# A two-block transformer on one core: the last attention group takes the middle token tiles of all heads first, and their feed-forward is queued between the outer tiles' attention

## The chip, the core and the metric

The kernel runs on one core of a Trainium2 chip. Its time is the device time of one execution in microseconds; the median of three runs is 643.6 (642.69 to 645.32). Times inside the kernel come from one profiled execution of it and are counted from the start of its span.

## The reference

x is 1024 tokens by 256 values. Four layers follow one another, each `x = x + f(layernorm(x))`: an attention over channels, a gated feed-forward with silu, a causal attention with 32 query heads of 64 and 8 key/value heads (rotary positions), and a feed-forward with quantised values and weights of -1, 0 and 1. The last two matter here:

```python
scores = jnp.where(causal, einsum('bhqd,bkhd->bhqk', xq, xk) * scale, -inf)
out = einsum('bhqk,bkhd->bqhd', softmax(scores), xv) @ wo           # the third layer
h = gelu(bitlinear(x, w_fc))                                        # the fourth layer, 256 -> 1024
x = x + bitlinear(h, w_proj)                                        # 1024 -> 256
def bitlinear(x, w):   # layer norm, quantised by the row's largest value, times ternary weights
    xn = layer_norm(x)
    return einsum('bsd,od->bso', absmax_quant(xn), ternarize_weights(w))
```

Both quantisations and both layer norms work on one token's row, so a token tile can go through the feed-forward as soon as its own x is complete, that is, when the output projections of all 32 heads have been added to it.

## The kernel before, in words

Tokens lie in eight tiles of 128. Every engine has its program written out in order (a `@block` per engine); semaphores are all that joins them, and each engine takes its own instructions strictly as written. The places where the order is set are the loops over `G` and the straight lists behind them.

The causal attention has 64 steps `G`, eight per key/value group `g`. A step takes two heads (pair `p` of the group) and two query tiles: part 0 is tile 4+r with 5+r key blocks, part 1 is tile 3-r with 4-r key blocks, nine blocks in all for each head, whatever r is (`of_step`, `blocks`). In a group, steps 0 to 3 take pair 0 with r = 0 to 3 and steps 4 to 7 take pair 1 in the same order. So a tile's heads are complete only in the second half of a group: the middle tiles (2 to 5, from r = 0 and 1) with step 5.

In a step PE computes the scores (`scores`, L1404), DVE the row maxima (L1005), ACT the exponentials (`exp_unit`, L661) and their rounding to fp16 (`p_high`, L670), POOL the rest (`p_low`, L497), SP issues two transposing DMAs (`pT_hi` at L376, `pT_lo` at L380, 18 blocks each), and three steps later PE multiplies with the values (`pv`, L1421 and L1425, 54 products), and DVE divides by the row sums (`normalise_o`, L1012, L1014). The table `JOBS` puts side work between the parts of a step: `q1t`, `kt`, `q0t` and `r` prepare the next group, `ot0` to `ot3` transpose the normalised outputs (PE L1436, ACT `oT_high` L642, DVE `oT_low` L1020; one `ot` covers two steps), `wo0` to `wo3` are the output projections (`out_project`, 12 products per tile pair j, all by the helper `product`, L1151) of the group before, added to x by DVE (`add_out`, L1026). `RING` assigns them two PSUM banks, 6 and 7, by turns; a job waits until the one two places ahead of it has been read (`emptied`). The weights of the projection are split in `wo_hi` (ACT L624) and `wo_lo` (POOL L476, between the halves of the last step's `p_low`).

Behind the loop PE has: pV of step 61, pV of 62, `ot2`, the projections j = 1 and 2 (tiles 2 to 5), pV of 63, `ot3`, the projections j = 0 and 3, then for the feed-forward four transposed y tiles (`x_transposes(3, ...)`, L1167), and a pipeline over tiles t: `fc(t)` is 8 products of 512 columns (L1151), 256 to 1024 values; ACT `gelu_of(t)` (L717), `centre(t)` (L725), `squares(t)` (L732); DVE quantises z (`tensor_reduce` L1131, then L1133 to L1135); PE `z_transposes(t)` (L1523); ACT `z_high` (L710) and DVE `z_low` (L1116) split the transposed z, and `pj(t)` is 16 products of 256 columns (L1151), whose result DVE adds to x (`result`, L1123, L1126). Buffers of gelu, z and zT are double, the one of the z transposes (banks 4 and 5) is single: `z_transposes(t)` waits for `z_low(t-1)`. POOL computes the means and inverse deviations (L455, L457, L529 to L537). PE's order there, with `fc` two tiles ahead of the transposes:

```python
            for t in range(NT):
                if t + 2 < NT:
                    fc(t + 2)
                z_transposes(t)
                if t >= 1:
                    pj(t - 1)
```

Before it DVE does the moments and the quantisation of y in halves of four tiles (`quantise`, L1077 to L1090), ACT `x_high` (L552) and DVE `y_low` (L1097) split the transposed y.

Of the kernel before, what the change touches and what calls it, by code (L numbers as in the profile page):

```python
# [31 lines left out]
def transformer_program(nc, x_in, wq_a, wk_a, wv_a, wo_a, w_gate_up, w_down,  # L32
# [97 lines left out]
    y = sb("y", 26, [NT, C], F32)  # L130
    yT_hi = sb("yT_hi", 34, [KC, T], F16)
# [33 lines left out]
    with ExitStack() as ctx:  # L165
# [117 lines left out]

        def owner(G, name):

            g = G // 8
            if name[:2] == "wo" or name in ("ot2", "ot3"):
                return g - 1
            return g if name[:2] in ("ot", "q1") else g + 1

        def job(G, slot):
# [3 lines left out]
            name = JOBS[G % 8][slot]  # L295
# [107 lines left out]
        def _(pool):  # L403
# [142 lines left out]
        @block.scalar
        def _(act):
# [1033 lines left out]
```

## Time and profile before

| | us |
|---|---|
| median of three runs | 643.6 |
| the profiled execution | 642.03 |
| its span | 640.2 |
| mean granted clock of TensorE, of full speed | 0.976 |
| PE busy | 573.9 |
| DVE / ACT / POOL busy | 462.9 / 436.1 / 453.3 |

The profiled execution's own time is its span and 1.8 us around it. "Releaser" in a row is what ended the idle time before an instruction. A chain of waits is read backwards from the last instruction: each piece is work that, had it been shorter, would have let the next begin earlier. PE's matmuls overlap, so a group of n of them starts its followers n times their spacing later, and a single one's mean is longer than that spacing.

### The profile page before, as it was taken

What the parts mean: (1) busy time and instruction counts of PE and PEld (TensorE: products, weight loads), DVE (VectorE), ACT (ScalarE), POOL (GpSimd) and SP (SyncE); (2) the same over time, 40 slices, a digit from 0 to 9 for tenths busy, and PEclk for the clock granted to TensorE, in tenths of its full rate; (3) what the DMA queues carried; (4) which work ended last, traced back from release to release, by engine and by line L of the source; (5) the groups of instructions that cost most, each with busy time, mean ns of one, the idle gap of its engine ahead of it and who ended that gap; (6) DMA issues with size and microseconds to landing.
All of it is one profiled execution on the core that took longest, in us unless ns stands there. A gap on an engine that the chain in (4) does not pass through costs nothing.

```text
span 640.2 us, 16852 instructions
## 1 busy us (share of the span) xinstructions
PE 573.9 (90%) x7136; PEld 485.6 (76%) x7136; DVE 462.9 (72%) x764; ACT 436.1 (68%) x600; POOL 453.3 (71%) x387
## 2 busy tenths in 40 slices
PE   6999999978889999999999999999999978674896
PEld 5878889857668888888787888888888767673475
DVE  4785766867668778777787877877787756518696
ACT  1624311368788797898888879779888878701794
POOL 5044435529999999998997998899799778533121
PEclk9999999999999999999999999999999989957899
DMA  8150004008999999999999999999999999960001
GB/s 286 57 184 0 2 22 87 1 22 148 174 187 209 186 200 191 185 186 196 197 191 186 189 180 202 194 188 193 186 188 171 184 193 186 184 132 1 1 25 42
DMA packets 317195, 91.79 MB, mean 143 GB/s; under 512 B 305984, under 2 KB 316224, under 8 KB 317120
## 3 DMA queue, kind: packets, MB, share of 16 engines
q1 hardware_dynamic: 317120, 90.72, 80.0%
q8 instruction: 56, 0.92, 0.5%
q14 instruction: 19, 0.16, 0.1%
HBM read 13.11 MB, written 1.05 MB: 22 GB/s over the span
## 4 chain that ended last, share of the span: by engine, by line
PE 34%; POOL 26%; DMA 16%; DVE 9%; SPq 6%; ACT 6%; issue 4%; POOLq 0%; ACTq 0%; DVEq 0%
POOL p_lo L497 19%; DMA pT_lo<-p_lo 15%; PE PS L1151 12%; SPq L376 4%; PE PS L1404 4%; PE PS L1284 3%; POOL roped L486 3%; PE PS L1421 3%; SPq L380 2%; POOL roped L483 2%; PE PS L1261 2%; PE PS L1266 2%; PE PS L1262 2%; DVE small L1005 2%; ACT probs L661 2%
## 5 line engine op out<-in xcount | busy, mean ns | idle before, releaser
L497 POOL TENSOR_TENSOR p_lo<-probs,p_hi 128x1280 f16<-128x1280 f32 (+7 forms) x128 | 303.7, 2393 | 38.4 <-DMA pT_lo<-p_lo 29.6
L661 ACT ACTIVATE probs<-PS,small 128x640 f32<-128x640 f32 (+7 forms) x256 | 173.9, 743 | 44.7 <-DVE small L1005 36.9
L1005 DVE TENSOR_REDUCE small<-PS 128x2 f32<-128x1280 f32 (+7 forms) x128 | 172.9, 1351 | 28.2 <-PE PS L1404 26.4
L670 ACT CAST p_hi<-probs 128x1280 f16<-128x1280 f32 (+7 forms) x128 | 145.4, 1160 | 6.3 <-DMA pT_hi<-p_hi 6.1
L1404 PE MATMUL PS<-k_hi,q_hi 64*128 64x512 f32 (+2 forms) x384 | 75.4, 387 | 12.8 <-ACT probs L661 10.2
L1421 PE MATMUL PS<-v_hi,pT_hi 128*128 128x65 f16 x1152 | 79.0, 195 | 1.1 <-DMA pT_hi<-p_hi 0.6
L1425 PE MATMUL PS<-v_lo,pT_hi 128*128 128x64 f16 x1152 | 78.9, 195 | 0.0
L1404 PE MATMUL PS<-k_lo,q_hi 64*128 64x512 f32 (+2 forms) x384 | 78.4, 401 | 0.0
L1421 PEld LDWEIGHTS PS<-v_hi,pT_hi 128*128 128x128 f16 x1152 | 73.6, 99 | 5.0 <-issue 2.7
L1425 PEld LDWEIGHTS PS<-v_lo,pT_hi 128*128 128x128 f16 x1152 | 72.6, 98 | 0.4
L1404 PE MATMUL PS<-k_hi,q_lo 64*128 64x512 f32 (+2 forms) x384 | 67.7, 346 | 0.0
L1404 PEld LDWEIGHTS PS<-k_hi,q_hi 64*128 64x128 f32 x384 | 36.9, 186 | 29.3 <-issue 13.6
L1421 PE MATMUL PS<-v_hi,pT_lo 128*128 128x65 f16 x1152 | 46.6, 195 | 12.7 <-DMA pT_lo<-p_lo 12.4
L1421 PEld LDWEIGHTS PS<-v_hi,pT_lo 128*128 128x128 f16 x1152 | 39.9, 99 | 15.1 <-DMA pT_lo<-p_lo 14.8
L1151 PE MATMUL PS<-wkq_hi,xnT_hi 128*128 128x320 f32 x128 | 43.9, 343 | 6.2 <-DVE t_sin L951 2.0
L486 POOL TENSOR_TENSOR roped<-t_cos,t_sin 128x256 f32<-128x256 f32 x64 | 47.4, 740 | 0.0
L461 POOL TENSOR_TENSOR hT_lo<-h,hT_hi 128x512 fp32r<-128x512 f32 x16 | 23.6, 1477 | 32.7 <-DVE hT_hi L863 32.7
L1151 PE MATMUL PS<-wo_hi,oT_hi 128*128 128x256 f32 x128 | 39.9, 312 | 4.5 <-DVE oT_lo L1020 3.9
L1012 DVE RECIPROCAL small<-PS 128x4 f32<-128x4 f32 x64 | 11.5, 180 | 44.6 <-PE PS L1421 44.5
L483 POOL TENSOR_TENSOR roped<-t_cos,t_sin 128x128 f32<-128x128 f32 x64 | 29.7, 464 | 16.0 <-DVE t_sin L951 16.0
L1404 PEld LDWEIGHTS PS<-k_hi,q_lo 64*128 64x128 f32 x384 | 37.1, 187 | 3.3
L1151 PE MATMUL PS<-wkq_lo,xnT_hi 128*128 128x320 f32 x128 | 39.5, 309 | 0.0
(196 smaller groups left out, 1347.9 us busy)
## 6 DMA issues: line engine op xcount, KB each, us to landing
wgu_nat<-L_ffn_w_gate_up SPq DMA_DIRECT2D x2, 1024.0 KB, 10.1
wkq_nat<-L_attn_wq SPq DMA_DIRECT2D x8, 256.0 KB, 3.3
wo_nat<-L_attn_wo SPq DMA_DIRECT2D x8, 256.0 KB, 3.6
x<-L_attn_x SPq DMA_DIRECT2D x4, 256.0 KB, 3.8
wdn_nat<-L_ffn_w_down SPq DMA_DIRECT2D x1, 1024.0 KB, 11.5
wfc_nat<-L_ffn_w_fc SPq DMA_DIRECT2D x1, 1024.0 KB, 6.6
wpj_nat<-L_ffn_w_proj SPq DMA_DIRECT2D x1, 1024.0 KB, 9.6
pT_hi<-p_hi SPq DMA_TRANSPOSE x64, 5.5
```

The lines of the kernel that those rows point to most:

```text
L376: sp.dma_start(pT_hi[G % 3][:], p16_hi[G % 2][:], transpose=True).then_inc(pT_hi_landed[G % 3], 16)
L461: nc.gpsimd.tensor_tensor(hT_lo[:, n, :], h32[:, n % 3, :], hT_hi[:, n, :].bitcast(F32), ALU.subtract).then_inc(h_lo_done, 1)
L483: nc.gpsimd.tensor_tensor(roped[:, t, 0:P].rearrange("p (h d) -> p h d", h=2), t_cos[b][:, 0:1, :].broadcast_to(both), t_sin[b][:, 0:1, :] ...
L486: nc.gpsimd.tensor_tensor(roped[:, t, P:3 * P], t_cos[b][:, 1:5, :].rearrange("p h d -> p (h d)"), t_sin[b][:, 1:5, :].rearrange("p h d -> ...
L497: nc.gpsimd.tensor_tensor(p16_lo[G % 2][:, cols], probs[G % 2][:, cols], p16_hi[G % 2][:, cols], ALU.subtract).then_inc(p_lo_done, 1)
L661: nc.scalar.activation(probs[G % 2][:, start:start + w], PS[:, src:src + w], ACT.Exp, bias=nmax[:, 4 * (G % 2) + u:4 * (G % 2) + u + 1]).t ...
L670: nc.scalar.copy(p16_hi[G % 2][:, cols], probs[G % 2][:, cols]).then_inc(p_hi_done, 1)
L1005: nc.vector.tensor_reduce(nmax[:, first:first + 2], both_heads(part)[:, :, 0:blocks(G, part) * P], AX.X, ALU.max, negate=True).then_inc(nm ...
L1151: last = nc.tensor.matmul(dst, lhsT, rhs, start=n == 0, stop=n == len(pairs) - 1)
L1404: last = nc.tensor.matmul(dst[a], q[rows_of[a], q_cols], k[rows_of[a], cols], start=m == 0, stop=m == 2)
L1421: last = nc.tensor.matmul(o[:, u:u + HEAD + 1], p_block, v_hi[:, j, g, :], start=first, stop=False, skip_group_check=True)
L1425: nc.tensor.matmul(o[:, u:u + HEAD], p_block, v_lo[:, j, g * HEAD:(g + 1) * HEAD], start=False, stop=False, skip_group_check=True)
```

## The change

In the last group the order of the steps becomes pair 0 r = 0, 1, pair 1 r = 0, 1, pair 0 r = 2, 3, pair 1 r = 2, 3. The middle tiles are complete with step 59 of the 64. The projections of the group before move to steps 59 and 60, `ot0` and `ot1` to 61 and 63, and the middle tiles' own projections (`po1`, `po2`) into step 63; `wo_lo` is split in step 62 and `wo_hi` in step 61. Behind the loop, the feed-forward of the middle tiles (t = 0 to 3 in the new order `TAIL_TILES`) is queued between the last pV, the last `ot` and the outer projections (`po0`, `po3`) on PE, ACT and DVE; the outer tiles (t = 4 to 7) follow. y and its transposes get other places in memory, gelu gets a semaphore of its own for its scale, the inverse deviations are computed for four tiles at once, and the scale of the result is computed by POOL instead of DVE. The bodies of `fc` and `z_transposes` stay, but for a wait of `fc(1)` that goes; `pj` takes its bank from the ring. The diff, cut to its core:

```diff
-    y = sb("y", 26, [NT, C], F32)
-    yT_hi = sb("yT_hi", 34, [KC, T], F16)
+    y = sb("y", 112, [NT, C], F32)
+    yT_hi = sb("yT_hi", 120, [KC, T], F16)
     yT_lo = sb("yT_lo", 38, [KC, T], F16)
...
         def of_step(G):
             g, n = G // 8, G % 8
+            if g == NG - 1:
+                return g, n, n // 2 % 2, 2 * (n // 4) + n % 2
             return g, n, n // 4, n % 4
 
         def blocks(G, part):
-            r = G % 4
+            r = of_step(G)[3]
             return 4 - r if part else 5 + r
 
...
+        LAST_JOBS = {0: ("q1t0", "q1t1", ""), 1: ("", "", "ot2"), 2: ("", "", ""), 3: ("ot3", "wo0", "wo1"),
+                     4: ("wo2", "wo3", ""), 5: ("ot0", "", ""), 6: ("", "", ""), 7: ("ot1", "po1", "po2")}
+        LAST_WO = (1, 2, 0, 3)
+        TAIL_TILES = (2, 3, 4, 5, 0, 1, 6, 7)
+
...
-            name = JOBS[G % 8][slot]
+            name = (LAST_JOBS if G >= STEPS - 8 else JOBS)[G % 8][slot]
             return name if name and 0 <= owner(G, name) < NG else ""
...
                     split_wo_low(g - 1)
-                if G == STEPS - 1:
+                if G == STEPS - 2:
                     split_wo_low(NG - 1)
                 p_low(G, 1)
 
-            for i in range(NT):
-                rstd(3, i, BIT_EPS)
+            def rstd_half(hf):
+
+                v = moments[:, 3, 8 * hf + 1:8 * hf + 8:2]
+                pool.wait_ge(moments_done, 3 * NT + 4 * hf + 4)
+                nc.gpsimd.tensor_scalar(v, v, BIT_EPS, None, ALU.add).then_inc(var_eps_done, 1)
+                pool.wait_ge(var_eps_done, 2 * NT + hf + 1)
+                nc.gpsimd.tensor_tensor(v, v, neg_half.broadcast_to([P, 4]), ALU.pow).then_inc(rstd_done, 1)
+
+            rstd_half(0)
...
+            def z_scale(t):
+                pool.wait_ge(z_rstd_done, t + 1)
+                pool.wait_ge(z_done, t + 1)
+                nc.gpsimd.tensor_scalar(bit[:, 7, t:t + 1], bit[:, 5, t:t + 1], bit[:, 10, t:t + 1],
+                                        ngam[:, 1:2], ALU.mult, ALU.mult).then_inc(z_scale_done, 1)
+
             for t in range(NT):
                 z_mean(t)
+                if t == 3:
+                    rstd_half(1)
                 if t:
                     z_rstd(t - 1)
+                if t >= 2:
+                    z_scale(t - 2)
             z_rstd(NT - 1)
+            z_scale(NT - 2)
+            z_scale(NT - 1)
...
+                if G == STEPS - 3:
+                    split_wo_high(NG - 1)
             p_high(STEPS - 1, 1)
-            split_wo_high(NG - 1)
+            nc.scalar.activation(col(58), s_sum[:, 0:1], ACT.Gelu)
             oT_high(NG - 1, 2, side_bank(STEPS + 1, "ot2"))
-            oT_high(NG - 1, 3, side_bank(STEPS + 2, "ot3"))
...
                 act.wait_ge(fc_done, t + 1)
+                act.wait_ge(gelu_scale_done, t // 4 + 1)
...
             gelu_of(0)
             centre(0)
+            gelu_of(1)
+            squares(0)
+            oT_high(NG - 1, 3, side_bank(STEPS + 2, "ot3"))
+            for t in (1, 2):
+                centre(t)
+                gelu_of(t + 1)
+                z_high(t - 1)
+                squares(t)
+            centre(3)
+            squares(3)
+            z_high(2)
             for c in range(KC):
-                x_high(3, 1, c, 6 + c)
-            for t in range(NT):
-                if t:
-                    centre(t)
+                x_high(3, 1, c, 2 + c)
+            gelu_of(4)
+            for t in range(4, NT):
+                centre(t)
                 if t + 1 < NT:
                     gelu_of(t + 1)
-                if t:
-                    z_high(t - 1)
+                z_high(t - 1)
                 squares(t)
             z_high(NT - 1)
...
+            def add_last(G, name):
+                j = int(name[-1])
+                add_out(4 * (NG - 1) + LAST_WO.index(j) + 1, j, side_bank(G, name))
...
             side(STEPS - 1, 2)
-            for G in range(STEPS, STEPS + PV_LAG):
-                normalise_o(G - PV_LAG, side_bank(G, "pv"))
-                if G == STEPS + 1:
-                    oT_low(NG - 1, 2, side_bank(G, "ot2"))
-                if G == STEPS + 2:
-                    oT_low(NG - 1, 3, side_bank(G, "ot3"))
...
+            def tail_moments(hf):
+
+                for t in range(4 * hf, 4 * hf + 4):
+                    if t % 2 == 0:
+                        dve.wait_ge(x_added, ADDS + t // 2 + 1)
+                    nc.vector.bn_stats(stats[:, 6 * t:6 * t + 6], x[:, TAIL_TILES[t], :]).then_inc(stats_done, 1)
+                    dve.wait_ge(stats_done, 3 * NT + t + 1)
+                    nc.vector.bn_aggr(moments[:, 3, 2 * t:2 * t + 2], stats[:, 6 * t:6 * t + 6]).then_inc(moments_done, 1)
...
+            def gelu_scale(hf):
+
+                tiles = slice(4 * hf, 4 * hf + 4)
+                dve.wait_ge(rstd_done, 2 * NT + hf + 1)
                 nc.vector.scalar_tensor_tensor(out=bit[:, 3, tiles], in0=bit[:, 1, tiles], scalar=ngam[:, 0:1],
-                                               in1=rstds[:, tiles, 1], op0=ALU.mult, op1=ALU.mult)
-
-            def y_low(hf):
+                                               in1=rstds[:, tiles, 1], op0=ALU.mult,
+                                               op1=ALU.mult).then_inc(gelu_scale_done, 1)
...
             def result(t):
 
-                dve.wait_ge(z_rstd_done, t + 1)
-                step(nc.vector.tensor_scalar(bit[:, 7, t:t + 1], bit[:, 5, t:t + 1], bit[:, 10, t:t + 1],
-                                             ngam[:, 1:2], ALU.mult, ALU.mult))
+                dve.wait_ge(z_scale_done, t + 1)
                 dve.wait_ge(pj_done, t + 1)
...
-                if t >= 2:
-                    result(t - 2)
+
+            tail_moments(0)
+            normalise_o(STEPS - 3, side_bank(STEPS, "pv"))
+            quantise(0)
+            normalise_o(STEPS - 2, side_bank(STEPS + 1, "pv"))
+            oT_low(NG - 1, 2, side_bank(STEPS + 1, "ot2"))
+            y_low(0, 4)
+            gelu_scale(0)
+            quantise_z(0)
+            normalise_o(STEPS - 1, side_bank(STEPS + 2, "pv"))
+            oT_low(NG - 1, 3, side_bank(STEPS + 2, "ot3"))
+            quantise_z(1)
+            add_last(STEPS + 2, "po0")
+            add_last(STEPS + 2, "po3")
+            z_low(0)
+            tail_moments(1)
+            quantise_z(2)
+            quantise(1)
+            z_low(1)
+            result(0)
+            y_low(1, 2)
+            gelu_scale(1)
+            for t in range(3, NT):
+                quantise_z(t)
+                z_low(t - 1)
+                result(t - 2)
             z_low(NT - 1)
             result(NT - 2)
             result(NT - 1)
...
 
                 pe.wait_ge(wo_split, gg + 1)
-                pe.wait_ge(oT_lo_done, 4 * gg + (3 if gg == NG - 1 and j in (1, 2) else 4))
...
             for G in range(STEPS):
...
             side(STEPS + 1, "pv")
             side(STEPS + 1, "ot2")
             pe.wait_ge(exp_done, 4 * STEPS)
-            out_project(NG - 1, 1, 1)
-            out_project(NG - 1, 2, 2)
+            x_transposes(3, 0, 4)
+            fc(0)
+            fc(1)
+            fc(2)
             side(STEPS + 2, "pv")
             side(STEPS + 2, "ot3")
-            out_project(NG - 1, 0, 0)
-            out_project(NG - 1, 3, 3)
-
-
-            x_transposes(3, 0, 4)
-
...
-            fc(0)
-            fc(1)
-            x_transposes(3, 1, 4)
-            for t in range(NT):
-                if t + 2 < NT:
-                    fc(t + 2)
-                z_transposes(t)
-                if t >= 1:
-                    pj(t - 1)
-            pj(NT - 1)
+            z_transposes(0)
+            fc(3)
+            side(STEPS + 2, "po0")
+            side(STEPS + 2, "po3")
+            z_transposes(1)
+            side(STEPS + 3, "pj0")
+            z_transposes(2)
+            side(STEPS + 3, "pj1")
+            pe.wait_ge(gelu_done, 4)
+            x_transposes(3, 1, 0)
+            for t in range(4, NT):
+                fc(t)
+                z_transposes(t - 1)
+                side(STEPS + 3, f"pj{t - 2}")
+            z_transposes(NT - 1)
+            side(STEPS + 3, f"pj{NT - 2}")
+            side(STEPS + 3, f"pj{NT - 1}")
```

## Rows read from the trace of the kernel before

**Rows 1.** The page, parts 1 and 2: busy time by engine; PE clock of 40 slices.
```profile
PE 573.9 (90%) x7136; PEld 485.6 (76%) x7136; DVE 462.9 (72%) x764; ACT 436.1 (68%) x600; POOL 453.3 (71%) x387
...
PEclk9999999999999999999999999999999989957899
```

**Rows 2.** The chain that ended last, 530 to 640: start us, us, what.
```profile
568.36 5.38 PE PS L1151 x24
...
578.35 1.69 PE PS L1151 x12
...
583.10 1.15 DVE y L1077 x4
...
591.46 6.54 PE PS L1151 x16
...
607.58 3.47 PE PS L1151 x24
611.06 0.87 PE PS L1523 x8
```

**Rows 3.** Timeline of POOL, last two steps: start us, us, instruction, idle before.
```profile
553.00 4.74 POOL L497 TENSOR_TENSOR p_lo<-probs,p_hi 128x1792 f16<-128x1792 f32 x2 [3.31 <-DMA pT_lo<-p_lo]
...
564.24 1.27 POOL L476 TENSOR_TENSOR wo_lo<-wo_nat,wo_hi 128x512 fp32r<-128x512 f32 x1
```

**Rows 4.** Timeline of DVE after the last attention step.
```profile
575.65 0.42 DVE L1014 TENSOR_TENSOR o<-PS,small 128x256 f32<-128x256 f32 x1
...
580.84 0.43 DVE L756 BATCH_NORM_STATS2 stats<-x 128x6 f32<-128x256 f32 x1
...
587.00 0.22 DVE L1090 SCALAR_TENSOR_TENSOR bit<-bit,small,moments 128x4 f32<-128x4 f32 x1
```

**Rows 5.** Timeline of ACT at the feed-forward's first tiles.
```profile
588.51 0.59 ACT L552 CAST yT_hi<-PS 128x512 f16<-128x512 f32 x1 [0.27 <-PE PS L1167]
...
595.07 1.11 ACT L717 ACTIVATE gelu<-PS,bit 128x1024 f32<-128x1024 f32 x1 [4.67 <-PE PS L1151]
...
596.64 1.15 ACT L725 ACTIVATE z<-gelu,bit 128x1024 f32<-128x1024 f32 x1 [0.36 <-POOL bit L529]
...
599.43 1.13 ACT L717 ACTIVATE gelu<-PS,bit 128x1024 f32<-128x1024 f32 x1
```

**Rows 6.** Groups by line, 591.4 to 638.3: busy us, mean ns, idle before.
```profile
L1131 DVE TENSOR_REDUCE bit<-z 128x1 f32<-128x1024 f32 x8 | 9.8, 1219 | 1.2 <-ACT z L725 0.9
L1116 DVE SCALAR_TENSOR_TENSOR zT_lo<-PS,zT_hi 128x1024 f16<-128x1024 f32 x8 | 9.7, 1218 | 1.6 <-ACT zT_hi L710 1.6
...
L717 ACT ACTIVATE gelu<-PS,bit 128x1024 f32<-128x1024 f32 x8 | 8.9, 1115 | 4.8 <-PE PS L1151 4.7
...
L710 ACT CAST zT_hi<-PS 128x1024 f16<-128x1024 f32 x8 | 8.1, 1008 | 2.7 <-PE PS L1523 2.7
...
L1135 DVE TENSOR_SCALAR z<-z,bit 128x1024 f32<-128x1024 f32 x8 | 6.0, 754 | 0.3
```

**Rows 7.** Timeline of PE, same stretch.
```profile
600.22 0.38 PE L1151 MATMUL PS<-fcT,yT_lo 128*128 128x512 f16 x1
602.73 1.09 PE L1523 MATMUL PS<-identf,z 128*128 128x128 f32 x8 [2.14 <-DVE z L1135]
603.66 0.38 PE L1151 MATMUL PS<-fcT,yT_hi 128*128 128x512 f16 x1
```

**Rows 8.** Half-microsecond stretches: us, busy by engine, granted clock, DMA share, GB/s.
```profile
557.00:557.50 0.50, 0.27 (x9) 0.15 (x5) 0.00 (x0) 0.50 (x1) 0.50 (x1) 1.00 1.07 184
559.50:560.00 0.50, 0.00 (x0) 0.00 (x0) 0.00 (x0) 0.00 (x0) 0.00 (x0) 0.86 0.66 146
573.50:574.00 0.50, 0.50 (x16) 0.45 (x16) 0.00 (x0) 0.00 (x0) 0.00 (x0) 0.99 0.00 0
581.00:581.50 0.50, 0.45 (x4) 0.25 (x3) 0.47 (x3) 0.00 (x0) 0.00 (x0) 1.00 0.00 0
583.50:584.00 0.50, 0.00 (x0) 0.00 (x0) 0.50 (x3) 0.00 (x0) 0.34 (x2) 0.75 0.00 0
```

More of the change, by code:

```diff
@@ L288, in owner @@
                 return g - 1
-            return g if name[:2] in ("ot", "q1") else g + 1
+            return g if name[:2] in ("ot", "q1", "po") else g + 1
         def job(G, slot):
@@ L302, in transformer_program @@
             RING += [(G, job(G, slot)) for slot in (1, 2) if job(G, slot)]
-        RING += [(STEPS, "pv"), (STEPS + 1, "pv"), (STEPS + 1, "ot2"), (STEPS + 2, "pv"), (STEPS + 2, "ot3")]
+        RING += [(STEPS, "pv"), (STEPS + 1, "pv"), (STEPS + 1, "ot2"), (STEPS + 2, "pv"), (STEPS + 2, "ot3"),
+                 (STEPS + 2, "po0"), (STEPS + 2, "po3")] + [(STEPS + 3, f"pj{t}") for t in range(NT)]
         def side_bank(G, name):
@@ L322, in both_heads, with o_cols @@
             return bank(first, 2 * (second - first)).rearrange("p (a n) -> p a n", a=2)
-        def o_cols(oT, m):
-            o = oT[:, m // 2, :]
-            if m % 2:
+        def o_cols(oT, gg, m):
+            p, outer = (m % 2, m // 2) if gg == NG - 1 else (m // 2, m % 2)
+            o = oT[:, p, :]
+            if outer:
                 return o.rearrange("p (a n) -> p a n", a=4)[:, 0::3, :]
@@ L641, in oT_high @@
                 act.wait_ge(oT_done, 4 * gg + m + 1)
-                nc.scalar.copy(o_cols(oT_hi, m), bank(b).rearrange("p (a n) -> p a n", a=2)).then_inc(oT_hi_done, 1)
+                nc.scalar.copy(o_cols(oT_hi, gg, m), bank(b).rearrange("p (a n) -> p a n", a=2)).then_inc(oT_hi_done, 1)
             def side(G, slot):
@@ L1075, in quantise @@
                 dve.wait_ge(moments_done, 3 * NT + 4 * hf + 4)
-                for i in range(4 * hf, 4 * hf + 4):
-                    last = nc.vector.tensor_scalar(y[:, i, :], x[:, i, :], mean_of(3, i), None, ALU.subtract)
-                    if i < 4 * hf + 3:
+                for t in range(4 * hf, 4 * hf + 4):
+                    last = nc.vector.tensor_scalar(y[:, t, :], x[:, TAIL_TILES[t], :], mean_of(3, t), None, ALU.subtract)
+                    if t < 4 * hf + 3:
                         steps[0] += 1
@@ L1384, in scores @@
                     pe.wait_ge(qk_lo_done, 6 * g + 4)
-                if n == 4 and part == 0:
+                if n == (2 if g == NG - 1 else 4) and part == 0:
                     pe.wait_ge(qk_lo_done, 6 * g + 6)
@@ L1441, in out_project @@
                 pe.wait_ge(wo_split, gg + 1)
-                pe.wait_ge(oT_lo_done, 4 * gg + (3 if gg == NG - 1 and j in (1, 2) else 4))
+                pe.wait_ge(oT_lo_done, 4 * gg + (2 if gg == NG - 1 and j in (1, 2) else 4))
                 for t in (2 * j, 2 * j + 1):
@@ L1479, in side @@
                     qk_transposes(name[:-2], owner(G, name), int(name[-1]), b)
-            for G in range(STEPS):
-                scores(G, 0)
-                scores(G, 1)
-                side(G, job(G, 0))
-                if G >= PV_LAG:
-                    side(G, "pv")
-                side(G, job(G, 1))
-                side(G, job(G, 2))
-            side(STEPS, "pv")
-            side(STEPS + 1, "pv")
-            side(STEPS + 1, "ot2")
-            pe.wait_ge(exp_done, 4 * STEPS)
-            out_project(NG - 1, 1, 1)
-            out_project(NG - 1, 2, 2)
-            side(STEPS + 2, "pv")
-            side(STEPS + 2, "ot3")
-            out_project(NG - 1, 0, 0)
-            out_project(NG - 1, 3, 3)
-            x_transposes(3, 0, 4)
             def fc(t):
```

73 lines of the change are left out of this document (41 added, 32 removed).

## Prediction

> **What bounds the kernel now.** I read the page first. No engine is full over the span, and the last eight of 40 slices differ from the rest: PE's clock falls there in three places [rows 1]. Then the chain of waits. Up to 568 it runs through the transposing DMAs and POOL's `p_lo`. From 568 it is a serial tail: output projections, x, y, its transposes, the first two `fc` at 591.46, and only from 607 an even pattern of `pj`+`fc` (3.47) and z transposes (0.87), 4.34 us a tile, PE against itself [rows 2]. Between 568 and 591 most engines wait for one another; that is what the change can win. The tail afterwards is eight tiles at 4.34, so the look-ahead that gives 4.34 must survive.
>
> Below, tile t is the t-th in the new order (token tiles 2, 3, 4, 5, 0, 1, 6, 7); clock times are those of the profiled span, and the attention part up to 553 keeps them.
>
> **Attention part.** Steps are reordered, but each still has nine blocks, two transposes of 18 blocks and the same queues, and `wo` jobs move into PE's idle time. I take 0 (bounds -1 and +3, three microseconds being two output projections at full clock, 1.69 each [rows 2], if they held up scores). `wo_lo` (1.27) moves from between the halves of the last `p_lo` to between those of the step before: `p_lo` of that step starts at 553.0, its first half takes 4.74 less the second's share (512 of 2304 columns, 1.05), so `wo_lo` ends at 553.0+3.7+1.27 = 558.0 [rows 3].
>
> **Way to the first fc.** `po1` and `po2` need that `wo_lo`: start 558.0. PE stood still for four microseconds before, so they run at the low clock, 5.4 for the two (the piece at 568.36 [rows 2]) (at full clock 3.4): 563.4. Then DVE in its queue: second add 0.75, 564.2; moments of four tiles 2.26 (580.84 to 583.10), 566.4; `normalise_o` 0.6, 567.0; `quantise(0)` 583.10 to 587.1, 4.0, 571.0 [rows 2, 4]. PE's y transposes and ACT's two copies end 2.0 later, as before (587.1 to 588.51+0.59), 573.0 [rows 4, 5]; the two `yT_lo` end 0.7 after the copy (half of a 1.2 pair), and `fc(0)` starts at 573.9. Before: 591.46. **Gain here 17.6** (20 with the fast clock, 14 if a queue slips). ACT's gelu table is loaded in its idle time before this, at no cost.
>
> **Edits taken at nothing.** The scale of the output moves from DVE to POOL (0.27 less on DVE per tile; POOL has only short work in the tail); the eight single `rstd` become two of four tiles, off the path by the quantisation that runs beside them; y and its transposes get another place; `gelu` waits for a scale that is there 0.2 after `yT_lo`, long before `fc(0)` ends; the output's eight DMAs are issued by SP in the new order with nothing else in its queue. If POOL's cover goes (it waits in order for `z_done` too), the price is one result late by 0.3.
>
> **Middle: tiles 0 to 3, with outer attention mixed in.** `fc(0)`, `fc(1)` again start on the low clock, 6.54: 580.4 [rows 2]. `gelu(0)` starts 3.6 after the first `fc`, 577.5, its centring 1.57 later, until 580.2 [rows 5]; the z quantisation on DVE is 1.22 for the maximum, 0.75 for the scaling [rows 6] and 0.4 for two instructions of one column, 2.4: 582.6. PE: `fc(2)` to 582.0, then `pv(63)`, 1.8 (36 products of the high half, 18 of the low), 583.8; normalise 0.6, transposes 0.7: 585.2. `oT_high(3)` is queued on ACT ahead of `centre(1)`, so ACT stands from 582.7 to 585.3 and everything behind it too. `centre(1)` ends at 586.9, z(1) on DVE at 589.4. PE does z transposes, `fc(3)`, `po0`, `po3` (2.9 at full clock) until 590.8. Now DVE is the bound, in its order: adds 591.7; `z_low(0)` 592.8; moments 594.9; quantise z(2) 597.3; `quantise(1)` 601.2; `z_low(1)` 602.4 (1.22 each for `z_low` [rows 6]). PE waits for that `z_low(1)` from 595.6, seven microseconds, so its clock is low when `z_transposes(2)`, `pj(1)` and the second y transposes run (1.8, 3.5, 1 after the clock rises): 608.3. ACT's copy and DVE's `yT_lo` add 1.5: `fc(4)` starts at **609.9** (607.7 on a fast clock). Before, `fc(4)` is the second half of the 607.58 piece: 609.2 [rows 2]. So of 17.6 nothing is left: +0.7. The overlap is there, but `pv`, transposes, two projections, ACT's stand and DVE's eleven stages in a row took it.
>
> **Tiles 4 to 7: the look-ahead.** Before, PE's order is `fc(t+2)`, `z_transposes(t)`, `pj(t-1)`; after, in the last loop, `fc(t)`, `z_transposes(t-1)`, `pj(t-2)`. ACT's order is the same in both: `centre(t)`, `gelu(t+1)`, `z_high(t-1)`, `squares(t)`. So on ACT `gelu(5)` stands ahead of `z_high(3)`, and on PE `fc(6)` stands behind `z_transposes(4)` and `pj(3)`, which need `z_low(3)`. That closes a ring: `fc` 1.94 to the start of gelu (8x0.216, its tail and a semaphore), gelu 1.09 to the next on ACT, `z_high` 1.01, `z_low` 1.23 and 0.15 of semaphores, z transposes 0.87, `pj` 1.75: **8.05 us from fc to fc** instead of 4.34 [rows 2, 6]. Before, `fc(6)` ran before the transposes of 4, so there was no ring. `fc(5)`: quantise z(3) after `yT_lo` and `z_low(2)` end at 613.6, transposes and `pj(2)` 2.7, 616.3. `fc(7)`: two rings, 632.4. Before it started near 622.2, three periods after 609.2. After `fc(7)` the end came 15.9 later (to 638.1), and the new order gives the same within 0.5 (two z chains one behind the other): 648.3, **+10.3** on a fast clock.
>
> **The clock in the ring.** In it PE works 4.35 and stands 3.6 in every round. The trace: idle since 581.4, the granted clock fell from 1.00 (2.4 GHz) in the stretch that starts at 583.50, 2.3 us later; after idling from 557.3 it fell before 560.0; it was given back at 573.5, 5.1 us after PE began to work without a break at 568.4 [rows 2, 8]. So I expect it to fall in most of three waits, and each fall to cost half of that 5.1 at 1.2 GHz, 2.5 (bounds 0 and 4.36, a whole round's work at half speed), the last one only 1, since the two last z chains hide it: six in all, and with some chance that one is missed **+5**. Together +15: this profiled execution took 642.0 (span 640.2 and 1.8 around it), so it would take 657.4; the median of the runs shown is 1.6 above it, so 643.6+15 = **658.6**.
>
> The Trainium skill (TensorE: Matmul & The Clock Gate, HAM oscillation) says that a kernel whose matmul bursts are parted by waits is throttled again in each wait and starts every burst cold; by it all three falls come, and the sum is about a microsecond higher; without it, at one clock, it is 5 lower. The rows at 559.5 and 583.5 side with it.
>
> **Rivals.** (a) *The ring closes, but the clock stays up*: PE's shorter wait of 2.1 at 600.6 did not lower it, and a wait of 3.6 may pass in the same way [rows 7]. +10.3: 654. (b) *The clock stays low through the ring*: each round has 4.36 more, three rounds 13, and the end 2: +25, 669. For it: 560 to 573.5 was low throughout; against: that stretch was broken by small waits, here ztr, `pj`, `fc` are 8.7 us without a break at 1.2 GHz. (c) *Faster*: PE lets ready products pass a waiting transpose, so that neither order nor ring binds. Then only the work counts: 17.6 gained less `pv` 1.8, transposes 0.7, projections 2.9: -12, 631.5. Against it: `gelu(1)` was done at 600.56 and `fc(3)` ready, yet PE stood until 602.73, did the z transposes and only then `fc(3)` at 603.66 [rows 5, 7]. The same page of the Trainium skill gives TensorE a queue of 64 with a partial reorder window, but in its step-by-step section only weight loads are pulled ahead, matmuls keep their order; by the first sentence alone it would be 631.5. (d) *No change*: middle as reckoned, ring broken because `fc` catches up: +0.7, 644. (e) *The change doesn't overlap*: `po1` is late (its `wo_hi`, behind the weight's load, or the attention order), y starts after the last pV; then `fc(0)` slips by up to ten and that shifts half of what follows: 668. The sign turns only if ring and middle together cost under 17.6 less what is won; the middle alone takes 18.3.
>
> **Chances.** Forecast 0.60, (a) 0.17, (b) 0.07, (c) 0.07, (d) 0.03, (e) 0.06. A measurement here tells 0.5%, 3.2 us, from no change. Faster by more: (c), 0.07; within: (d), 0.03; slower 0.90. The range 650 to 666 has the forecast's own bounds (falls 0 to 3, middle from 2.2 less) and (a).
>
> **What would show it.** `fc(0)` near 574; ACT idle before its second last `oT_hi`; PE idle some 7 us before the third z transposes, ended by `zT_lo`; `fc(5)` to `fc(7)` 8 to 11 apart with DVE's `zT_lo` releasing PE and PE releasing ACT's gelu; PEclk dips in the last three slices. Wrong if the last `fc` come 4 to 5 apart, or if `fc(4)` starts before 600.

## The result, and the profile after it

The changed kernel takes **657.2 us** (median of 4 runs, 653.73 to 661.3) against 643.5 for the kernel before (4 runs beside it, 642.69 to 645.32). The ratio is 1.0215 [1.0189, 1.0242], so it is 13.7 us slower; the forecast was 15 slower, 658.6. The profiled execution took 659.01, its span is 657.2 and the mean granted clock 0.969 (before: 642.03, 640.2 and 0.976).

The page after, its lines of busy time and of PE's clock in 40 slices, answers to [rows 1]:

```profile
PE 580.9 (88%) x7136; PEld 489.0 (74%) x7136; DVE 460.4 (70%) x756; ACT 436.5 (66%) x601; POOL 452.1 (69%) x383
...
PEclk9999999989999999999999999999999988877978
```

PE has the same 7136 products and is busy 7.0 us longer: the same work at a lower clock. Before, four of the last eight slices are under 9, after, seven of eight: 33 to 37, and 39 and 40, where the last two thirds of the ring lie.

The chain that ended last, of the kernel after (start us, us, what), answers to [rows 2]:

```profile
558.39 2.42 POOL p_lo L508
...
561.94 1.27 POOL wo_lo L487
...
563.31 4.59 PE PS L1217 x24
...
577.71 8.29 PE PS L1217 x24
...
606.08 1.94 PE PS L1573 x8
608.02 3.27 PE PS L1217 x16
...
623.16 0.91 ACT zT_hi L741
624.10 1.24 DVE zT_lo L1159
...
625.47 1.94 PE PS L1573 x8
627.41 5.55 PE PS L1217 x24
...
634.19 0.91 ACT zT_hi L741
635.12 1.23 DVE zT_lo L1159
...
636.49 1.07 PE PS L1573 x8
637.56 3.49 PE PS L1217 x24
```

Read it downwards. Projections `po1`, `po2` stand at 563.31 and three `fc` in a row at 577.71, where `fc` began at 591.46 before. Then, from 623, the chain hops from ACT to DVE to PE and back, twice with the same stations. In [rows 2] that stretch is PE against itself, 3.47 and 0.87, with no other engine in it.

ACT's timeline of the kernel after (start us, us, instruction, idle time before and what ended it) answers to [rows 5]:

```profile
581.32 1.11 ACT L749 ACTIVATE gelu<-PS,bit 128x1024 f32<-128x1024 f32 x1 [4.60 <-PE PS L1217]
...
589.14 0.59 ACT L672 CAST oT_hi<-PS 128x512 fp32r<-128x512 f32 x1 [2.49 <-PE PS L1502]
...
615.74 1.11 ACT L749 ACTIVATE gelu<-PS,bit 128x1024 f32<-128x1024 f32 x1 [2.90 <-PE PS L1217]
...
621.96 1.11 ACT L749 ACTIVATE gelu<-PS,bit 128x1024 f32<-128x1024 f32 x1 [3.51 <-PE PS L1217]
...
632.98 1.11 ACT L749 ACTIVATE gelu<-PS,bit 128x1024 f32<-128x1024 f32 x1 [6.74 <-PE PS L1217]
...
641.07 1.11 ACT L749 ACTIVATE gelu<-PS,bit 128x1024 f32<-128x1024 f32 x1 [3.80 <-PE PS L1217]
```

The last four gelu begin at 615.74, 621.96, 632.98 and 641.07: 6.2, 11.0 and 8.1 apart. Before, they began at 611.12, 615.44, 619.79 and 624.13, 4.34 apart; the first and the last of them in ACT's timeline of the kernel before:

```profile
611.12 1.11 ACT L717 ACTIVATE gelu<-PS,bit 128x1024 f32<-128x1024 f32 x1
...
624.13 1.11 ACT L717 ACTIVATE gelu<-PS,bit 128x1024 f32<-128x1024 f32 x1
```

PE's timeline of the kernel after shows the other side of the same ring (rows of [rows 7] answer to it):

```profile
606.08 1.94 PE L1573 MATMUL PS<-identf,z 128*128 128x128 f32 x8 [4.97 <-DVE zT_lo L1159]
...
617.38 1.06 PE L1573 MATMUL PS<-identf,z 128*128 128x128 f32 x8 [1.68 <-DVE zT_lo L1159]
...
625.47 1.94 PE L1573 MATMUL PS<-identf,z 128*128 128x128 f32 x8 [3.55 <-DVE zT_lo L1159]
...
636.49 1.07 PE L1573 MATMUL PS<-identf,z 128*128 128x128 f32 x8 [3.55 <-DVE zT_lo L1159]
...
644.58 1.41 PE L1573 MATMUL PS<-identf,z 128*128 128x128 f32 x8 [3.55 <-DVE zT_lo L1159]
```

In the ring, behind `fc(5)`, `fc(6)` and `fc(7)`, PE waits 3.55 for `zT_lo` ahead of the z transposes, and behind the first two of these waits `fc` of the next tile, whose operands are ready, is queued. Of the five transposes shown two take 1.94 (low clock) and two 1.06 or 1.07 (full clock); in the last, 1.41, the clock falls.

From such rows comes the whole account of the profiled execution, between points that both kernels have:

| stretch | before | after | difference |
|---|---|---|---|
| to `p_lo` of the 7th step from the end (57) | 521.47 | 522.39 | +0.9 |
| from there to `p_lo` of the last step but one (62) | 31.5 | 36.0 | +4.5 |
| to `fc(0)` | 38.5 | 19.3 | −19.1 |
| `fc(0)` to gelu(4) | 19.7 | 38.0 | +18.4 |
| gelu(4) to gelu(7) | 13.0 | 25.3 | +12.3 |
| gelu(7) to the last result | 13.9 | 14.0 | +0.1 |
| sum | 638.1 | 655.1 | +17.0 |

The profiled execution of after lies 1.8 above its median and that of before 1.5 below its own; the rest is the 13.7.

### The profile page after: what moved, and what is told of

Same layout as the page of the kernel before. It is cut to its first block, busy times and chain, and to the rows that moved or that the text cites. A ratio compares the mean times of both kernels' runs of the same rounds, so it can differ in the third digit from the quotient of the medians.

```text
span 657.2 us, 16853 instructions
## 1 busy us (share of the span) xinstructions
PE 580.9 (88%) x7136; PEld 489.0 (74%) x7136; DVE 460.4 (70%) x756; ACT 436.5 (66%) x601; POOL 452.1 (69%) x383
## 4 chain that ended last, share of the span: by engine, by line
PE 31%; POOL 29%; DMA 17%; DVE 9%; issue 5%; ACT 4%; SPq 4%; POOLq 0%; ACTq 0%; DVEq 0%
POOL p_lo L508 22%; DMA pT_lo<-p_lo 16%; PE PS L1217 12%; POOL roped L497 3%; PE PS L1350 3%; PE PS L1470 3%; POOL roped L494 2%; SPq L386 2%; PE PS L1327 2%; PE PS L1332 2%; PE PS L1328 2%; PE PS L1487 2%; PE PS L1573 1%; PE PS L1240 1%; SPq L390 1%
## 5 line engine op out<-in xcount | busy, mean ns | idle before, releaser
L508 POOL TENSOR_TENSOR p_lo<-probs,p_hi 128x2048 f16<-128x2048 f32 (+7 forms) x128 | 303.8, 2395 | 40.4 <-DMA pT_lo<-p_lo 24.3
L691 ACT ACTIVATE probs<-PS,small 128x128 f32<-128x128 f32 (+7 forms) x256 | 173.7, 742 | 50.7 <-DVE small L1047 42.3
L1047 DVE TENSOR_REDUCE small<-PS 128x2 f32<-128x2048 f32 (+7 forms) x128 | 172.8, 1350 | 28.3 <-PE PS L1470 26.7
L700 ACT CAST p_hi<-probs 128x2048 f16<-128x2048 f32 (+7 forms) x128 | 145.5, 1160 | 5.4 <-DMA pT_hi<-p_hi 5.2
L1470 PE MATMUL PS<-k_hi,q_hi 64*128 64x512 f32 (+2 forms) x384 | 75.1, 386 | 15.3 <-ACT probs L691 12.7
L494 POOL TENSOR_TENSOR roped<-t_cos,t_sin 128x128 f32<-128x128 f32 x64 | 29.9, 468 | 17.1 <-DVE t_sin L993 17.0
L1217 PE MATMUL PS<-wkq_hi,xnT_lo 128*128 128x320 f32 x128 | 39.5, 308 | 0.0
```

The lines of the kernel that those rows point to most:

```text
L494: nc.gpsimd.tensor_tensor(roped[:, t, 0:P].rearrange("p (h d) -> p h d", h=2), t_cos[b][:, 0:1, :].broadcast_to(both), t_sin[b][:, 0:1, :] ...
L508: nc.gpsimd.tensor_tensor(p16_lo[G % 2][:, cols], probs[G % 2][:, cols], p16_hi[G % 2][:, cols], ALU.subtract).then_inc(p_lo_done, 1)
L691: nc.scalar.activation(probs[G % 2][:, start:start + w], PS[:, src:src + w], ACT.Exp, bias=nmax[:, 4 * (G % 2) + u:4 * (G % 2) + u + 1]).t ...
L700: nc.scalar.copy(p16_hi[G % 2][:, cols], probs[G % 2][:, cols]).then_inc(p_hi_done, 1)
L1047: nc.vector.tensor_reduce(nmax[:, first:first + 2], both_heads(part)[:, :, 0:blocks(G, part) * P], AX.X, ALU.max, negate=True).then_inc(nm ...
L1217: last = nc.tensor.matmul(dst, lhsT, rhs, start=n == 0, stop=n == len(pairs) - 1)
```

## The experiments

Nine kernels. Each time stands beside runs of the kernel before on the same chip.

**e1: the look-ahead put back.** In PE's last loop `fc(t+1)` is issued ahead of the z transposes of t-1.

```
+            fc(4)
             for t in range(4, NT):
-                fc(t)
+                if t + 1 < NT:
+                    fc(t + 1)
                 z_transposes(t - 1)
```

> The changed kernel with one thing put back: in the last loop PE does fc(t+1) ahead of z_transposes(t-1), as before the change; ACT's and DVE's orders stay. Theory (the ring of fc, gelu, z_high, z_low, z transposes and pj costs 8.05 us per tile instead of 4.34, and its waits lower the clock): fc(4) starts where it did (613.8), fc(6) to fc(7) come 4.3 apart, fc(7) starts near 624.4 instead of 639.1, the end follows 15.9 later, so 10 (on a fast clock) to 14.8 us (against the profiled execution) go: about 645. Rival (the tail is bound by the amount of work on PE, ACT and DVE or by the outer attention's lateness, not by PE's order): under 3 us, 654 or more.

Measured: 641.8 (10 runs, 639.24 to 647.48; before 643.4), ratio 0.9991 [0.9962, 1.0019]. ACT's timeline of e1, the last gelu:

```profile
620.69 1.10 ACT L749 ACTIVATE gelu<-PS,bit 128x1024 f32<-128x1024 f32 x1
...
624.90 1.11 ACT L749 ACTIVATE gelu<-PS,bit 128x1024 f32<-128x1024 f32 x1
```

The last three gelu have no idle time before them, and these two are 4.2 apart. gelu(4) to gelu(7) takes 11.0 in place of 25.3. Moving one call in one engine's order gives back all of the loss: the ring is shown, and so is what closes it. It also speaks against products that pass a waiting transpose; if they did, this edit would change nothing.

**e2: the ring cut on ACT instead.** ACT copies `z_high(t-1)` before it does `gelu_of(t+1)`; PE's order is that of the change.

```
                 centre(t)
+                z_high(t - 1)
                 if t + 1 < NT:
                     gelu_of(t + 1)
-                z_high(t - 1)
```

> The changed kernel with PE's order as it is, but in ACT's last loop z_high(t-1) stands ahead of gelu_of(t+1). Theory of the ring: it is cut at another link. What is left is the longer chain fc, gelu, mean, centring, z quantisation, z_low, z transposes, pj, fc over two tiles, 11.0 for two, 5.5 us a tile instead of 8.05; waits of PE are then 1 to 2 us and the clock stays up: 5 to 9 us less than the changed kernel, 648 to 652. Rival (only fc being ahead helps, ACT's order is neutral since ACT is idle most of the tail): within 2 us of the changed kernel, 655 to 659.

Measured: 649.8 (647.79 to 652.93), ratio 1.0109 [1.007, 1.0148]. ACT's timeline of e2:

```profile
623.44 1.11 ACT L749 ACTIVATE gelu<-PS,bit 128x1024 f32<-128x1024 f32 x1 [2.46 <-PE PS L1217]
...
628.21 1.11 ACT L749 ACTIVATE gelu<-PS,bit 128x1024 f32<-128x1024 f32 x1 [0.50 <-PE PS L1217]
...
635.10 1.11 ACT L749 ACTIVATE gelu<-PS,bit 128x1024 f32<-128x1024 f32 x1 [2.46 <-PE PS L1217]
```

Two tiles take 4.77+6.89 = 11.7 (11.0 reckoned) in place of two rounds of 8.1, which fits a ring that closes once in two tiles, over the whole chain of z. Half of e1's gain is there, as reckoned. The ring needs both orders, PE's and ACT's.

**e3: the clock alone.** Twelve products of 512 columns whose result nobody uses run after `fc(t)` for t = 5, 6, 7, in PE's wait.

```
                 fc(t)
+                if t > 4:
+                    pe.wait_ge(gelu_done, t)
+                    for n in range(12):
+                        nc.tensor.matmul(bank(2 * ((t + 1) % 2)), fcT[:, 0, 0, :],
+                                         pjT[:, 0, 0:4, :], start=True, stop=True)
                 z_transposes(t - 1)
```

> The changed kernel with 12 products of 512 columns that nothing uses, on PE between fc(t) and z_transposes(t-1) for t = 5, 6, 7, where PE waited 3.6 us; they take 2.6 us and write to a bank that is free there. If the falls of the clock in the ring's waits cost time (forecast: 5 us; the profiled execution showed one whole round of 11.0 instead of 8.1 and a slow piece in the last, 3 to 4 us), the clock is 1.00 from fc(5) on, every round is 8.1, and the kernel is 2 to 5 us faster although PE has 7.8 us more to do: 652 to 655, with less spread between runs. Rival (the clock's falls are hidden behind the other engines in the ring): no change, or slower by what the products add, 657 to 660.

Measured: 652.5 (651.03 to 655.25), ratio 1.0152 [1.0122, 1.0182]. PE's timeline of e3 in the wait that lasts from 621.9 to 625.5 in the changed kernel:

```profile
618.98 2.75 PE L1615 MATMUL PS<-pjT,fcT 128*128 128x512 f16 x12
622.69 1.06 PE L1573 MATMUL PS<-identf,z 128*128 128x128 f32 x8 [0.96 <-DVE zT_lo L1159]
```

PE idles 0.96 and its transposes take 1.06. Gelu 5, 6 and 7 begin at 619.18, 627.26 and 635.35: rounds of 8.08 and 8.09, the ring at full clock. With some 8 us more work on PE the kernel is 4.7 faster by the medians and 4.1 by the ratios, whose intervals do not meet. So the falls in the ring cost some 4 to 5 in the median; the rest of what e1 gives back is the order's.

**e4: the same ring in the kernel before.** There is no overlap with attention in it; only PE's order changes.

```
-            for t in range(NT):
-                if t + 2 < NT:
-                    fc(t + 2)
-                z_transposes(t)
-                if t >= 1:
-                    pj(t - 1)
+            z_transposes(0)
+            for t in range(2, NT):
+                fc(t)
+                z_transposes(t - 1)
+                pj(t - 2)
+            z_transposes(NT - 1)
+            pj(NT - 2)
```

> The kernel before with one thing changed: PE's order in the tail is fc(t), z_transposes(t-1), pj(t-2), as in the changed kernel's last loop, for t = 2 to 7; attention and everything else stay. Theory of the ring: fc(2) starts after z_transposes(0) at 603.6 instead of 598.7, five rounds of 8.05 instead of 4.34 follow, the end comes 15.9 after fc(7): 21.7 us slower on a fast clock, with falls of the clock in the waits up to 32 slower: 665 to 676. Rival (the ring is particular to the changed order with its late second half): under 8 us slower.

Measured: 673.0 (672.05 to 673.98), ratio 1.0464 [1.0442, 1.0486], 29.6 slower. ACT's timeline of e4, two of its last six gelu:

```profile
637.63 1.11 ACT L717 ACTIVATE gelu<-PS,bit 128x1024 f32<-128x1024 f32 x1 [5.48 <-PE PS L1151]
...
645.71 1.11 ACT L717 ACTIVATE gelu<-PS,bit 128x1024 f32<-128x1024 f32 x1 [3.81 <-PE PS L1151]
```

The rounds are 9.7, 9.8, 9.8, 8.1 and 9.8 us. The shortest is the ring at full clock; the others are 1.7 longer, each with a fall. So the ring alone, in another kernel, costs 3.7 to 5.4 a tile.

**e5: the projections' place in attention.** The changed kernel does `wo0` and `wo1` back to back in one step; here three steps share them: `wo0`; `wo1` and `wo2`; `wo3`.

```
-        LAST_JOBS = {..., 3: ("ot3", "wo0", "wo1"), 4: ("wo2", "wo3", ""), 5: ("ot0", "", ""), ...}
+        LAST_JOBS = {..., 3: ("ot3", "wo0", ""), 4: ("wo1", "wo2", ""), 5: ("ot0", "wo3", ""), ...}
```

> The changed kernel with the four output projections of the group before spread over steps 59 to 61 (wo0; wo1, wo2; wo3) instead of two in each of 59 and 60. In the profiled execution wo0 and wo1 ran back to back from 531.3 to 535.7 ahead of the scores of step 60, half of it at the low clock, and the first fc came 3.8 us later than forecast (577.7 for 573.9). Theory (this row of projections held up the scores): the first half of the last-but-one p_lo starts 2 to 5 us earlier, and the kernel is 2 to 4 us faster than the changed one: 653 to 655. Rival (the lateness comes from the step order itself, or the clock's fall at 549.8 while PE waits for the exponentials of step 61): within 1 us, 656 to 658.

Measured: 652.2 (650.6 to 655.71; before 644.2), ratio 1.0135 [1.0098, 1.0172]. Against after's ratio that is 0.8%, some 5 us, more than expected. The trace shows less: the stretch that was 36.0 is 33.7 here, and the last result is 3.3 earlier than after's. The five kernels with the changed job table show 33.5 to 36.3 for it, the three with this one 32.2 to 33.7 (median 34.6 and 33.5), so the traces give the move one to three, and the pair back to back was only a part of the lateness; the four runs of after spread by more than what is left open. `wo0` still stands in step 59 here.

**e6: the queue on DVE.** `z_low(1)`, for which PE waits, goes ahead of the quantisation of the second y half.

```
-            quantise(1)
             z_low(1)
+            quantise(1)
```

> The changed kernel with one swap on DVE: z_low(1) ahead of quantise(1) instead of behind it. Theory (DVE's order is the bound between tile 1 and fc(4); PE waited from 597 to 606.1 for that z_low): z_transposes(2) starts at 602.2 instead of 606.1, quantise(1) ends 1.1 later than before and no longer last, fc(4) comes 3 to 4 us earlier: 653.5. Rival (the outer y, ready at 604.8 before and 605.9 now, is the bound for fc(4)): 1 us or less, 656 or more.

Measured: 653.1 (651.74 to 653.49; before 644.2), ratio 1.0138 [1.0116, 1.0161]. PE's timeline of e6 at the third z transposes:

```profile
602.92 1.07 PE L1573 MATMUL PS<-identf,z 128*128 128x128 f32 x8 [1.07 <-DVE zT_lo L1159]
```

The wait of 4.97 (from 601.1; the expectation has it from 597, but `z_transposes(1)` and `pj(0)` ran in between) is 1.07, and the transposes run at full clock. From gelu(0) to gelu(4) it is 28.9 in place of 34.4; of that 5.5 the median keeps 4 to 5.

**e7: e1, e5 and e6 together.**

> Three edits together: fc ahead in the last loop, z_low(1) ahead of quantise(1), the projections spread. If they act at different places their gains add: 641.8 (fc ahead alone) less 3.5 less 3: 635, 1.2% under the kernel before. If the spread projections do nothing, 638; if they share one bound, 641.

Measured: 637.3 (634.83 to 638.87; before 644.2), ratio 0.9893 [0.9861, 0.9925]. In the traces the three add: the ring 14.4 less, the middle 5.8 less, `fc(0)` 2.5 earlier, 22.6 in all by the last result. By the ratios the single gains sum to 24.5 and together they give 20.7. Each single gain is taken against after's four runs, which lie 7.6 apart; whether the missing four are more than that spread stays open. The measured 637.3 lies between the expectation's 635, if all three add, and its 638, if the spread projections do nothing, so this run does not show that they add in the median.

**e8: e7, with the last pV ahead of the first fc.** Its transposes (`ot3`) follow the first `fc`, its projections the third. ACT copies `ot3` ahead of centring tile 0, and DVE normalises ahead of quantising it. PE's part of the edit, against e7, without the rest:

```
             x_transposes(3, 0, 4)
+            side(STEPS + 2, "pv")
             fc(0)
+            side(STEPS + 2, "ot3")
             fc(1)
             fc(2)
-            side(STEPS + 2, "pv")
-            side(STEPS + 2, "ot3")
-            z_transposes(0)
-            fc(3)
             side(STEPS + 2, "po0")
             side(STEPS + 2, "po3")
+            z_transposes(0)
+            fc(3)
```

> The three edits of e7_all, and the outer attention earlier: pv(63) on PE before fc(0), in the wait for the y split (its last transposes had landed by then), ot3 behind fc(0), po0 and po3 behind fc(2) and before the first z transposes; ACT copies ot3 before centring tile 0, DVE normalises before z(0). Theory (ACT's stand of 2.5 us before oT_hi and DVE's row of adds, moments and quantisation behind it are latency of the outer attention mixed in too late): fc(4) comes 4 to 5 us earlier than in e7_all, 629 to 632. Rival (DVE's amount of work between fc(0) and fc(4) is the bound, whatever its order): within 1.5 us of e7_all, 634 to 636.

Measured: 631.8 (628.53 to 634.12; before 644.2), ratio **0.9794 [0.9758, 0.983]**, the fastest version, 12.4 below the kernel before. PE's timeline of e8, all its waits that ended with a z transposes before 606:

```profile
591.49 1.06 PE L1573 MATMUL PS<-identf,z 128*128 128x128 f32 x8 [1.04 <-DVE zT_lo L1159]
...
597.03 1.06 PE L1573 MATMUL PS<-identf,z 128*128 128x128 f32 x8 [2.73 <-DVE zT_lo L1159]
```

The last pV fills PE's wait for `yT_lo` ahead of `fc(0)`, its transposes no longer wait, and ACT's stand of 2.49 is gone. From gelu(0) to gelu(4) it is 24.1 (28.6 in e7).

**e9: the order of the steps alone.** The kernel before, with the last group's steps in the changed order, its own job table and its own tail. The edit also takes `blocks`, the columns that an `ot` fills and one wait for `qk_lo` along to the new order; its core:

```
+            if g == NG - 1:
+                return g, n, n // 2 % 2, 2 * (n // 4) + n % 2
             return g, n, n // 4, n % 4
...
```

> The kernel before with the last group's step order of the changed kernel and nothing else: its side jobs, its tail and its feed-forward stay. In the profiled executions the last-but-one p_lo started 31.5 us after the p_lo of step 57 before, 36.0 in the changed kernel, 33.7 with its projections spread. Theory (the lateness comes from where the projections and ot jobs stand, the step order itself is free, since every step has nine blocks): 643 to 645, the distance 31 to 32. Rival (the order costs by itself, by the sizes of the parts that follow one another, the 2.2 us that the spreading did not give back): 645.5 to 646.5, the distance 33 or more.

Measured: 643.9 (12 runs, 642.35 to 645.02; before 644.2, 16 runs), ratio 0.9996 [0.9983, 1.001]. POOL's timeline of the kernel after, then that of e9 (the same three steps, `p_lo` of two halves each):

```profile
534.91 4.74 POOL L508 TENSOR_TENSOR p_lo<-probs,p_hi 128x1536 f16<-128x1536 f32 x2 [1.59 <-DMA pT_lo<-p_lo]
545.11 4.70 POOL L508 TENSOR_TENSOR p_lo<-probs,p_hi 128x1792 f16<-128x1792 f32 x2 [5.46 <-ACT p_hi L700]
...
558.39 3.59 POOL L508 TENSOR_TENSOR p_lo<-probs,p_hi 128x1792 f16<-128x1792 f32 x1 [2.24 <-ACT p_hi L700]
```

```profile
534.25 4.75 POOL L500 TENSOR_TENSOR p_lo<-probs,p_hi 128x1536 f16<-128x1536 f32 x2 [1.58 <-ACT p_hi L673]
539.44 4.72 POOL L500 TENSOR_TENSOR p_lo<-probs,p_hi 128x1792 f16<-128x1792 f32 x2 [0.44 <-ACT p_hi L673]
...
552.41 4.73 POOL L500 TENSOR_TENSOR p_lo<-probs,p_hi 128x1792 f16<-128x1792 f32 x2 [1.87 <-DMA pT_lo<-p_lo]
```

With the order alone, two steps' `p_lo` follow 5.2 apart; with the changed job table 10.2, since POOL stood 5.46 waiting for ACT. The order alone costs nothing that 12 runs show. From step 57 to step 62 the changed kernel needs 36.0 and e9 30.8; 5.0 of these 5.2 arise between the `p_lo` of steps 59 and 60, where the two kernels differ by the jobs alone. `wo_hi`, which also moved, is split on ACT only at 551.25. What came late came from the jobs laid between the steps.

## Why the prediction was right, point by point

**Attention part: mis-sized.** I took 0, with 3 as the upper bound; in the profiled execution it is +4.5 (36.0 for 31.5), and 2.0 to 4.8 over five kernels with that job table. The step that failed is "`wo` jobs move into PE's idle time". I priced two projections at 1.69 each at full clock. PE's timeline of the kernel after shows `wo0`+`wo1` from 531.32 to 535.7, the second half at the low clock, ahead of the scores that start at 535.74:

```profile
531.32 0.36 PE L1217 MATMUL PS<-wo_hi,oT_hi 128*128 128x256 f32 x1 [1.92 <-issue]
...
533.05 0.41 PE L1217 MATMUL PS<-wo_hi,oT_hi 128*128 128x256 f32 x1
...
535.74 0.57 PE L1470 MATMUL PS<-k_hi,q_hi 64*128 64x512 f32 x2
```

ACT's exponentials, its `p_hi` and POOL's `p_lo` wait for those scores. The 1.92 of idle time before `wo0` is a second part that I had not seen. The code has `out_project` wait for `wo_lo`, and POOL makes it between the halves of the `p_lo` of step 58. POOL's timeline of the kernel after:

```profile
529.96 1.25 POOL L487 TENSOR_TENSOR wo_lo<-wo_nat,wo_hi 128x512 fp32r<-128x512 f32 x1
```

It ends at 531.21, and `wo0` starts 0.11 later. In all eight kernels that have `wo0` in step 59, e5 too, it starts 0.10 to 0.11 after `wo_lo` ends, and PE has stood idle for 0.4 to 2.2 before it. Of the five with the changed table, the two that stood 1.9 (after and e2) have the longest stretches, 36.0 and 36.3, the three that stood 0.4 to 0.5 (e1, e3, e6) 33.5 to 34.6. So PE was idle there, but the projection was not ready. e9, with `wo0` a step later, shows that the order is free and that the jobs' places hold the whole of the lateness; e5 gives back only a part. How it divides between the wait for `wo_lo` and the row of projections was not tried by an edit of its own.

**Way to the first fc.** From `p_lo` I said 20.9; it took 19.3. Of the 1.6, 0.8 is `po1` and `po2` (4.59, not 5.4), 0.4 the way from the end of `quantise(0)` to `fc(0)` (2.5, not 2.9), the rest tenths. With the lateness above, `fc(0)` came at 577.7 and not at 573.9: the gain is 13.8, not 17.6.

**Middle: right.** From `fc(0)` to `fc(4)` I said 36.05; it took 36.1 (577.71 to 613.82). That it fits to a tenth is in part luck: the terms 1.8, 3.5 and 1 of the forecast add up to 6.3, where it went on with 5.9 (measured 5.7), and ACT's copy and `yT_lo` took 2.1, not 1.5. The stations are those of the text: ACT idle 2.49 before its second last `oT_hi` (2.6 said), DVE's queue of two z chains, moments, y and its quantisation, and PE idle 4.97 before the third z transposes (some 7 said; the `pj(0)` before it ran at the low clock and ended later). DVE's timeline of the kernel after shows the queue ahead of `zT_lo`, and e6 that it was this queue:

```profile
601.99 1.22 DVE L1132 TENSOR_REDUCE bit<-y 128x4 f32<-128x1024 f32 x1
...
603.66 1.14 DVE L1137 TENSOR_SCALAR y<-y,bit 128x256 f32<-128x256 f32 x4
604.72 1.22 DVE L1159 SCALAR_TENSOR_TENSOR zT_lo<-PS,zT_hi 128x1024 f16<-128x1024 f32 x1
```

**Ring: right to the tenth.** 8.05 was worked out from single durations; the undisturbed rounds are 8.09 in the changed kernel, 8.08 and 8.09 in e3, 8.08 in e4, 8.09 in e5 and in e6. Without the clock gelu(4) to gelu(7) is 6.2 + 8.1 + 8.1 = 22.4, 9.4 more than before; I had said 9.6.

**The clock: right in kind, a little too dear.** I expected falls in most of three waits at 2.5 each and 1 for the last, 5 in all. The stretches of one microsecond of the kernel after (us, busy by engine, granted clock, DMA share, GB/s) answer to [rows 8]:

```profile
624.00:625.00 1.00, 0.00 (x0) 0.00 (x0) 0.90 (x1) 1.00 (x2) 0.00 (x0) 0.84 0.00 0
625.00:626.00 1.00, 0.53 (x3) 0.56 (x4) 0.71 (x2) 1.00 (x3) 0.63 (x2) 0.50 0.00 0
...
635.00:636.00 1.00, 0.00 (x0) 0.00 (x0) 0.88 (x1) 1.00 (x2) 0.00 (x0) 1.00 0.00 0
...
645.00:646.00 1.00, 1.00 (x8) 0.88 (x6) 0.61 (x1) 0.35 (x1) 0.56 (x2) 0.58 0.29 98
```

PE is idle from 621.9 on; between 624 and 625 the clock goes from 1.00 (2.4 GHz) to 0.50 (1.2 GHz). In the next wait, equally long, it keeps 1.00 at 635 to 636. After the third it falls just as PE has begun again (0.58 at 645 to 646). The one fall that lengthens a round cost 2.9 (11.0 for 8.1); the last one shows nothing in the stretch from gelu(7) to the last result, where I had put 1: it is 14.0 here and 14.0 in e3, at full clock. e3 gives the price over several runs, 4 to 5. Over all kernels with unfilled waits of 3.55 (after, e5 and e6 with three each, e4 with six) the clock fell in the wait, or within 1.2 behind it, 11 times of 15; each of the four kernels has one wait without a fall. The Trainium skill (TensorE: Matmul & The Clock Gate, HAM oscillation) has every burst start cold that follows such a wait. The traces agree on where the loss lies, not on that it is paid each time.

**Rivals.** (a), a clock that stays up, is what e3 forces; in the changed kernel itself it happened in one wait of three. Its argument, that the wait of 2.1 at 600.6 had not lowered the clock, does not carry: in the changed kernel PE waits 2.07 before the transposes at 596.64, and the clock falls right behind (0.68 from 597 to 598). (b), low throughout, is out: the rows at 636.49 and 637.56 are at full speed. (c) is out by e1. The Trainium skill (TensorE: Matmul & The Clock Gate, Step-by-step) has matmuls in program order; the runs agree, 15 us hang on that order. (d) would have needed e1's order. (e) came true in small part: `po1` started 5.3 later than said (563.3 for 558.0), and `fc(0)` slipped by 3.8.

**The sum.** Forecast −17.6 +18.3 +9.6 +5 = 15.3. Measured in the profiled execution: +5.4 (attention, with 0.9 of plain offset) −19.1 +18.4 +9.4 +2.9 +0.1 = 17.1. The term that I had wrong by most, attention (5.4 too small), was two thirds made up by the clock (3.0 for 5) and by the way to `fc(0)` (19.1 gained for 17.6). That the median's 13.7 is within 1.3 of the forecast's 15 owes something to this, and something to the runs: the four lie 7.6 apart, and the profiled one alone gives 17.0. The mechanism of the middle and of the ring is not luck; the closeness of the number is in part.

## What to carry to other kernels

When work is moved to overlap, write down for the stage behind it which engine's next item stands behind which wait: an order on PE and an order on ACT, each harmless, close a ring together, and its period is the sum of all stations instead of the longest (8.1 against 4.3 here). Keep one product group ahead of the waiting transposes; that single call was worth 15 us, and with it, with DVE's queue sorted by who waits for it and with the last pV taken earlier, the overlap became a gain of 2.1% (e8). Moved jobs need a price at the low clock and ahead of whatever they are put in front of, even where the engine looks idle, and what they read must be ready at the new place: here `wo_lo` was not.

## What the runs showed of the hardware

The granted clock does not fall in every wait of the same length: 3.55 us of idle PE lowered it in one place and not in the next, in one execution, 11 times of 15 in all. Nor does a shorter wait spare it: it fell behind 2.07 us in the changed kernel (597 to 598) and did not behind 2.14 in the kernel before (602.73). Unused products in the ring's waits made the kernel 4.7 faster.

The changed kernel's four runs lie 7.6 us apart, four of the kernel before 2.6. The ring's waits do not explain that: e1 has none of them, and its ten runs lie 8.2 apart; e4 has six, and its four lie 1.9 apart. What makes the spread stays open.
